# Sorted experts of a fused transformer step: rows loaded from ACT's queue, five raw weight places, results scattered to token rows per tile, the shared down product in two halves

## The reference, cut to what matters

```python
logits = xf @ router_w
probs = jax.nn.softmax(logits, axis=-1)
topw, topi = jax.lax.top_k(probs, K)                      # K = 2 of E = 8
combine = zeros((n, E)).at[arange(n)[:, None], topi].add(topw)
h = silu(einsum('nd,edf->nef', xf, w1))                   # w1, w2: 8 x 512 x 512
ye = einsum('nef,efd->ned', h, w2)
routed = einsum('ne,ned->nd', combine, ye)
gate, up = split(xf @ shared_gate_up)
shared = sigmoid(xf @ shared_gate_w) * ((silu(gate) * up) @ shared_down)
x = x + routed + shared
```

## Time and profile before

| | us |
|---|---|
| median of three runs (1823.58 to 1836.29) | 1834.05 |
| the profiled execution, its own time | 1833.97 |
| its span (first to last instruction) | 1832.2 |
| PE busy over the span | 1648.9 (90%) |
| DVE busy | 941.8 (51%) |
| ACT busy | 646.2 (35%) |
| first product of the tile loop starts | 1606.73 |
| last product of the tile loop ends | 1799.08 |

### The profile page before, as it was taken

One profiled execution on the slowest core, in us unless ns is written; L12 is line 12 of the kernel. 1 busy time (PEld: TensorE's weight loads), 2 busy tenths in 40 slices (PEclk: granted clock), 3 DMA queues, 4 the chain that ended last, 5 costly groups with the idle time before them and its releaser, 6 DMA issues.

```text
span 1832.2 us, 37869 instructions
## 1 busy us (share of the span) xinstructions
PE 1648.9 (90%) x16852; PEld 1324.9 (72%) x16852; DVE 941.8 (51%) x1370; ACT 646.2 (35%) x1138; POOL 139.8 (8%) x144
## 2 busy tenths in 40 slices
PE   4988789999888999988999999999989888778887
PEld 3733677887666788877888888888777666666765
DVE  4331774336336465563555555555551465566765
ACT  2212053234434321123333333333325112366761
POOL 1200520001000000030000000000021000300003
PEclk9999899999889899999999999999989899999999
DMA  5198001111100111111111111111111000589884
GB/s 206 59 372 323 3 24 52 46 47 52 47 25 4 47 47 46 52 55 46 54 53 54 54 54 54 54 42 36 44 37 47 30 4 2 195 301 326 298 296 155
DMA packets 60129, 171.43 MB, mean 94 GB/s; under 512 B 6432, under 2 KB 23328, under 8 KB 49600
## 3 DMA queue, kind: packets, MB, share of 16 engines
q1 hardware_dynamic: 57408, 160.62, 25.3%
q0 software_dynamic: 2560, 8.39, 1.4%
HBM read 150.57 MB, written 18.35 MB: 92 GB/s over the span
## 4 chain that ended last, share of the span: by engine, by line
PE 72%; DVE 10%; issue 6%; ACT 5%; DMA 5%; POOL 2%; SPq 1%; POOLq 0%; DVEq 0%; ACTq 0%
PE PS L775 20%; PE PS L777 19%; PE PS L776 19%; DMA pool_area<-xs_dram 3%; PE PS L1151 2%; PE PS L1006 2%; PE PS L1120 2%; PE PS L882 1%; PE PS L903 1%; DVE Wl L1727 1%; PE PS L1153 1%; DVE bns L1662 1%; PE PS L1135 1%; ACT Wh L1290 1%; ACT SCP L1324 1%
## 5 line engine op out<-in xcount | busy, mean ns | idle before, releaser
L775 PE MATMUL PS<-T1h,Wh 128*128 128x512 f32 x512 | 208.6, 408 | 23.6 <-DVE T1l L1740 11.7
L776 PE MATMUL PS<-T1l,Wh 128*128 128x512 f32 x512 | 205.7, 402 | 0.0
L777 PE MATMUL PS<-T1h,Wl 128*128 128x512 f32 x512 | 205.6, 402 | 0.0
L1727 DVE TENSOR_TENSOR Wl<-W,Wh 128x2048 fp32r<-128x2048 f32 x58 | 132.8, 2291 | 109.8 <-ACT Wh L1290 109.8
L1290 ACT CAST Wh<-W 128x2048 fp32r<-128x2048 f32 x58 | 110.7, 1910 | 121.9 <-PE PS L777 110.9
L1600 POOL TENSOR_TENSOR rs<-ve,half 128x1 f32<-128x1 f32 (+1 forms) x64 | 46.8, 731 | 1386.3 <-DVE ve L1677 1060.3
L775 PE MATMUL PS<-CTh,Wh 128*128 128x256 f32 x512 | 148.0, 289 | 0.6 <-ACT SCP L1488 0.6
L776 PE MATMUL PS<-CTl,Wh 128*128 128x256 f32 x512 | 144.6, 282 | 0.0
L777 PE MATMUL PS<-CTh,Wl 128*128 128x256 f32 x512 | 144.5, 282 | 0.0
L775 PEld LDWEIGHTS PS<-T1h,Wh 128*128 128x128 f32 x512 | 100.5, 196 | 46.6 <-DVE T1l L1740 12.8
L2083 DVE COPY pool_area<-PS 128x512 f32<-128x512 f32 x64 | 44.3, 691 | 165.7 <-PE PS L777 165.7
(11 more groups left out here) (319 smaller groups left out, 3365.2 us busy)
## 6 DMA issues: line engine op xcount, KB each, us to landing
W<-units_dram SPq DMA_DIRECT2D x58, 1024.0 KB, 5.1
pool_area<-units_dram SPq DMA_DIRECT2D x23, 1024.0 KB, 6.5
pool_area<-ctx_t_dram SPq DMA_DIRECT2D x32, 512.0 KB, 4.0
T1f<-ctx_dram SPq DMA_DIRECT2D x25, 512.0 KB, 6.6
H<-ctx_t_dram SPq DMA_DIRECT2D x15, 516.0 KB, 7.9
T1f<-ctx_t_dram SPq DMA_DIRECT2D x12, 516.0 KB, 7.8
xs_dram<-pool_area SPq DMA_DIRECT2D x23, 256.0 KB, 2.3
pool_area<-xs_dram SPq DMA_DIRECT2D x23, 256.0 KB, 5.5
```

What stands on the lines that cost most here:

```text
L775: nc.tensor.matmul(out_, a[0], b[0], start=first, stop=False)
L776: nc.tensor.matmul(out_, a[0], b[1], start=False, stop=False)
L777: return nc.tensor.matmul(out_, a[1], b[0], start=False, stop=last)
L1727: nc.vector.tensor_tensor(low_w(u), raw(u), high_w(u).bitcast(F32), ALU.subtract).then_inc(w_split, 1)
```

## The change

What it does:

1. **Rows.** The tiles of rows are loaded by DMAs that ACT issues (`load_tile`), each right after ACT's high part of the tile that had the place. ACT, no longer SP, waits for the scatters to land.
2. **Raw places.** Five in place of four (NRAW = 5): the fifth is `SCP`. The high and low places stay four. The loads of the loop's second, third and fourth unit wait for DVE's last low part of `su` instead of its last product.
3. **Results.** POOL scatters each result tile to `yt_dram`, row by row, to row k*1024 + token. For that, the slots have to know their tokens: DVE computes `idx2` (five small instructions), POOL scatters 16 times 128 entries of 8 bytes into `meta_dram` and loads them back as `of_slot`. Padding slots go to rows of their own.
4. **End.** SP waits for the last scatter and loads the two results of all tokens in 8 DMAs of 512 KB (into `H` and `pool_area`); DVE then does 16 weighted additions. The 16 gathers are gone.
5. **Down product.** `5.down` is loaded twice: once ahead of the loop, for token tiles 0 to 3 between `su` and the first tile, and once more at the end for tiles 4 to 7.
6. **Ahead of the loop.** `pos` comes one piece of `sg` earlier on PE, and ACT's two small exponentials come three silu pieces earlier, with one ACT_TABLE_LOAD more there and the one inside the loop's first tile gone.

The core of the diff:

```diff
+NRAW = 5
+    for t in range(TG):
+        J.add(("os", t), "dve", unit="5.down")
     J.add(("xt", 0), "dve", split=True)
...
-    for t in range(T):
-        J.add(("os", t), "dve", unit="5.down")
+    for t in range(TG, T):
+        J.add(("os", t), "dve", unit="5.down.again")
...
+        W6s = SCP[:, :, :]
...
+        def raw_slot(u):
+            return u % NW if u < TILE0 else (u - TILE0 + 1) % NRAW
...
             def load_unit(u):
-                if before_in_slot(u) is not None:
-                    sp.wait_ge(w_split, before_in_slot(u) + 1)
+                if earlier(u, raw_slot) is not None:
+                    sp.wait_ge(w_split, earlier(u, raw_slot) + 1)
                 elif u >= TILE0:
-                    sp.wait_ge(tmp_ready, tmps["su", G - 1, C - 1])
+                    sp.wait_ge(dve_drained, J.drain["su", G - 1, C - 1][1])
...
             sp.wait_ge(eid_ready, 1)
-            for k in range(NW6):
-                load_unit(TILE0 + k)
-            sp.wait_ge(scattered, 16 * TOP * T)
-            for i in range(NXS):
-                load_tile(i)
-            for k in range(NW6, 2 * NW6):
-                load_unit(TILE0 + k)
-            for i in range(NT + 1):
-                if i >= 1:
-                    load_tile(i + NXS - 1)
...
-                    store_tile(i - 1)
...
+            for u in range(TILE0, len(UNITS)):
+                load_unit(u)
+            for n in range(NYS):
+                sp.wait_ge(ys_out[n], 16 * len(range(n, NT, NYS)))
+            sp.wait_ge(w_split, len(UNITS))
+            for t in range(0, T, 2):
+                for k, dst in enumerate((H, A2t)):
+                    src = yt_dram[k * TOK + t * P:k * TOK + (t + 2) * P, :].rearrange("(t p) d -> p t d", p=P)
+                    sp.dma_start(dst[:, t:t + 2, :], src).then_inc(y_in[t // 2], 16)
...
+            act.wait_ge(scattered, 16 * TOP * T)
+            for i in range(NXS):
+                load_tile(i)
+            for k in range(2):
                 split_high(TILE0 + k)
...
                 if i + 1 < NT:
                     high_tile(("xt", i + 1), XTh, i + 1)
+                    load_tile(i + 1 + NXS)
...
+            for t in range(T):
+                for k in range(TOP):
+                    nc.gpsimd.indirect_dma_start(slots, bass.IndirectOffsetOnAxis(idx2[:, k, t:t + 1], 0),
+                                                 whose[:, k, t, :], None).then_inc(meta_scattered, 16)
+            pool.wait_ge(meta_scattered, 16 * TOP * T)
+            nc.gpsimd.dma_start(of_slot[:, :, :], meta_dram.rearrange("p (i n) -> p i n", n=2)).then_inc(of_slot_in, 16)
+            pool.wait_ge(of_slot_in, 16)
+            for i in range(NT):
+                pool.wait_ge(act_drained, y_copied(i))
+                nc.gpsimd.indirect_dma_start(yt_dram, bass.IndirectOffsetOnAxis(of_slot[:, i, 0:1], 0),
+                                             YS[:, i % NYS, :], None).then_inc(ys_out[i % NYS], 16)
```

More of the change, by code:

```diff
@@ L112, in tile_order @@
     return order + [("w2", NT - 1)]
-UNITS += [f"6.{w}.{i}" for w, i in tile_order()] + ["5.down"]
-DOWN_ROW = TILE0
-EXPERT_ROW = TILE0 + 1
+UNITS += [f"6.{w}.{i}" for w, i in tile_order()] + ["5.down.again"]
+EXPERT_ROW = TILE0
 UNIT = {name: i for i, name in enumerate(UNITS)}
@@ L431, in build @@
         drained = {"act": act_drained, "dve": dve_drained}
-        w_full = [sem(f"w_full{i}") for i in range(NW6)]
+        w_full = [sem(f"w_full{i}") for i in range(NRAW)]
+        whose_in = sem("whose_in")
+        whose_ready = sem("whose_ready")
+        meta_in = sem("meta_in")
+        meta_zeroed = sem("meta_zeroed")
+        meta_scattered = sem("meta_scattered")
+        of_slot_in = sem("of_slot_in")
+        y_in = [sem(f"y_in{i}") for i in range(T // 2)]
+        x_done = sem("x_done")
         zero_made = sem("zero_made")
@@ L441, in build @@
         ys_out = [sem(f"ys_out{i}") for i in range(NYS)]
-        gathered = [sem(f"gathered{i}") for i in range(T)]
-        gather_used = sem("gather_used")
         small_high = sem("small_high")
@@ L581, in slot, with earlier @@
         def slot(u):
[L583 removed]
+            return u % NW if u < TILE0 else (u - TILE0 + 1) % NW6
+        def raw_slot(u):
+            return u % NW if u < TILE0 else (u - TILE0 + 1) % NRAW
+        def earlier(u, place):
+            return max((v for v in range(u) if place(v) == place(u)), default=None)
         def fills(u):
[L587 to L590 removed]
+            return sum(raw_slot(v) == raw_slot(u) for v in range(u + 1))
         def before_in_slot(u):
[L594 to L596 removed]
+            return earlier(u, slot)
         def raw(u):
[L599 to L600 removed]
+            s = raw_slot(u)
+            return W[:, s, :, :] if s < NW else W6[:, s - NW, :, :] if s < NRAW - 1 else W6s
         def high_w(u):
@@ L1232, in _, with shared_out @@
                 feature_major(("su",), w, T1, g)
+            def shared_out(unit, tokens):
+                w = wait_unit(unit)
+                for t in tokens:
+                    wait(("su", t // TG, C - 1))
+                    token_major(("os", t), w, B1, t)
+            shared_out("5.down", range(TG))
             def transpose_rows(key, src):
@@ L1266, in _ @@
                     transpose_rows(("mt", i), HS[:, i % NHS, :])
-            w = wait_unit("5.down")
-            for t in range(T):
-                wait(("su", t // TG, C - 1))
-                token_major(("os", t), w, B1, t)
+            shared_out("5.down.again", range(TG, T))
         @block.scalar
@@ L1577, in _ @@
             high_tile(("xt", 0), XTh, 0)
+            load_tile(NXS)
+            for k in range(2, NW6):
+                split_high(TILE0 + k)
             for i in range(NT + 1):
@@ L2151, in _ @@
             last_slot, both, first_slot = (tiny[:, 8, i * T:(i + 1) * T] for i in range(3))
-            slot_w = [tiny[:, 9, k * T:(k + 1) * T] for k in range(TOP)]
+            part_of, cell = tiny[:, 9, 0:TOP * T], tiny[:, 10, 0:TOP * T]
+            slot_w = [tiny[:, 13, k * T:(k + 1) * T] for k in range(TOP)]
             dve.wait_ge(dis_in, 16)
@@ L2197, in _ @@
             low_tmp(("su", G - 1, C - 1), B1, (A_, C - 1, grp(G - 1)), G * C - 1)
-            for k in range(NW6):
-                split_low(TILE0 + k)
             def low_tile(key, pair, i):
                 low(key, pair, (A_, i % 2, A_))
+            split_low(TILE0)
+            for t in range(2):
+                weighted(("os", t), t, E)
+            split_low(TILE0 + 1)
+            for t in range(2, TG):
+                weighted(("os", t), t, E)
             low_tile(("xt", 0), (XTh, XTl), 0)
+            for k in range(2, NW6):
+                split_low(TILE0 + k)
             for i in range(NT + 1):
```

118 lines of the change are left out of this document (65 added, 53 removed).

## The result

| | before | changed |
|---|---|---|
| time, median (lowest to highest), same chip | 1835.17 us (1823.58 to 1842.43), 4 runs | 1789.80 us (1788.70 to 1792.57), 4 runs |
| ratio, 95% interval | 1 | 0.9737 (0.9707 to 0.9766) |
| profiled execution: its time, its span | 1833.97, 1832.2 us | 1792.57, 1789.6 us |
| lead: last row factor on POOL to first m1 | 62.2 us | 64.7 us |
| loop: first m1 to last matmul of m2 | 191.9 us (8.34 a tile) | 151.7 us (6.60 a tile) |

The kernel became 2.6% faster, 45 us, where 27 us (1834 to 1807) was forecast; the time lies 2 us under the range.

A forecast was written before the change was run, and what follows sets the result against it. Rows issued late behind SP's waits bound the loop, with the DMA engines next. 1833.97 + 1.4 (units) - 19 (loop) - 3 (after the last load) - 6.6 (end) gave 1806.8, say 1807 us; range 1792 to 1827.

The forecast's parts named there:

- The ring: Tile loop: SP issues rows only behind a unit waiting for a split; PE waited 46.9 us for rows.
- the loop's -19: Tile loop: 173 us of full DMA work at a share of 1, against 192; range -6 to -25 us.
- the rival at 1792 us: Tile loop: engines run at 388 GB/s and PE's 6.5 to 6.9 us a tile set the pace; chance 0.13.
- its units' wait: Start of the loop's loads: units wait for the last low part of `su` instead of the last product, +1.4 us.
- the stretch after the last load: Last tile: rows already there, last weights set the end, about 11.5 us where it was 14.4: -3 us.
- The first m1, priced at nothing: Ahead of the loop: added split and down products fall into gaps, first m1 stays at about 1606.7, no cost.
- The end: Last product to end of span: 33.1 us falls to 26.5, with 16 additions of 0.75 us; -6.6 us.
- The fifth place, priced at nothing by itself: Raw weight places in the loop: four would still be enough, so nothing, up to a few us of share.
- ACT's issue of the rows: Tile loop: at 0.43 us a load no cost; at 1.5 us the loop loses 9 us of its gain.
- The small scatters' work on the engines: Building the slots' list: 2048 packets of 8 bytes take 1.4 to 6.9 us of full work; +3 us taken.
- The rival at 1855 us: Small scatters are late, result scatters queue behind them and ACT stops at the fourth copy; chance 0.06.
- The rival of no change: Tile loop: engines stay at 0.87, the rows' wait becomes an equal units' wait; 1827 to 1833 us; chance 0.30.

The follow-up runs named there:

- the three edits of before: The kernel before with one edit each: rows on ACT's queue (1804.06 us), rows a tile earlier on SP's queue (1796.44 us), five raw places (1809.27 us).
- the run with less work for PE: The changed kernel with only the first of three partial products of each tile's matmuls, all loads, splits and copies kept: 1780.65 us, loop 148.1 us.
- the try with shared additions: Changed kernel with raw places reordered to load the second unit earlier, and four of 16 final additions moved to ACT and POOL: 1791.81 us, end 29.7 us.

## Why the prediction was wrong, and where it was right

**The ring: right.** Rows were late because of where SP could issue them. Asking for them a tile earlier on the same queue gave 38.3 of the 40.2 us. The forecast had put the cure in the queue as well as in the time; the runs say that it is the time.

**The step that failed: 306 / 0.87 = 352 GB/s as what a full share moves.** The prediction read the share of the DMA engines as a filling level that bytes follow in proportion. From it came 7.3 us a tile, "the DMA engines come next, ahead of ACT, PE and DVE", and the loop's -19. Block 0, in the prediction's own rows, had already moved more than that, 388 GB/s. With 415 GB/s, a tile's 2.62 MB take 6.3 us, less than PE's 6.43, and PE sets the loop: that is the rival at 1792 us, to which I had given a chance of 0.13. The trace of before could have told it. These are windows of one microsecond in its loop (columns as above), three with the engines at work on several transfers, three of another kind:

```profile
1654.00:1655.00 1.00, 1.00 (x6) 0.83 (x5) 1.00 (x2) 1.00 (x1) 0.00 (x0) 1.00 0.98 412
1656.00:1657.00 1.00, 0.24 (x2) 0.24 (x3) 1.00 (x1) 0.60 (x1) 0.00 (x0) 1.00 1.18 135
1661.00:1662.00 1.00, 1.00 (x6) 0.82 (x5) 1.00 (x1) 1.00 (x2) 0.00 (x0) 1.00 1.01 426
1676.00:1677.00 1.00, 1.00 (x4) 0.81 (x3) 0.33 (x1) 0.64 (x1) 0.00 (x0) 0.50 0.99 406
1680.00:1681.00 1.00, 1.00 (x6) 0.82 (x5) 0.40 (x1) 1.00 (x1) 0.00 (x0) 1.00 0.63 107
1685.00:1686.00 1.00, 1.00 (x8) 0.85 (x7) 1.00 (x1) 0.75 (x2) 0.00 (x0) 1.00 1.08 143
```

A share of about 1 goes with 406 to 426 GB/s and with 135 to 143. (Of the 92 windows of one microsecond from 1594 to 1786 with a share of 0.95 or more, 49 moved over 400 GB/s and 11 under 250; a packet is counted whole in the window in which it starts.) In the second kind SP had just issued two transfers, from half a microsecond ahead of the window to its start (1655.53 and 1655.91, 1679.70 and 1680.08, 1684.53 and 1684.92): engines count as busy with packets that hardly move yet. That it is the start-up of a transfer on an empty pool is my reading of the order in time; no run here tests it. What is shown is that the average over 192 us mixed the two kinds, that the division by 0.87 left the second kind in, and that in the changed kernel's steady part it is nearly gone (1.01 and 408 GB/s).

The times of single packets in the traces confirm the size. In before's loop (1594 to 1786 us) most packets of 8 KB took 0.309 us, but 853 of 5764 took over 0.355, half of these 0.57 us or more. What these took beyond 0.309 us is 0.12 of the share; without it the 306 GB/s filled 0.74 of the engines, not 0.87, and that is 413 GB/s for a full share (142 us of full work where the prediction had 167). The same sum over the loops (from 1610 us on) of the changed kernel, the one with rows back on SP's queue and the three edits of before gives 411 to 414 GB/s each time. In the changed kernel's steady part only 105 of 3581 packets were slow. Why they are slow stays open.

The objection that I had raised against the rival, a fifth of the bytes in rows of 2 KB, cost little: a packet of 2 KB took 0.084 us, 9% more for its bytes than one of 8 KB, and with these rows in the mix the engines still gave 412 to 417.

The Trainium skill's page "Perfetto Trace Analysis" (Identifying the Most-Contended Engine) warns of just this: for the DMA take the throughput, since occupancy over 16 engines misleads. Its section Roofline names some 435 GB/s of the 16 engines together as the limit of a single active core. The runs agree with both: no 90 us of any run moved more than some 420 GB/s. The figure of about 358 GB/s that the prediction took from the Trainium skill's page "DMA: Bandwidth & Descriptors" (Specifications) lies below what was measured.

**The sum, term by term.** From the last row factor on, 44.9 us were gained where 27.2 were forecast: 17.7 more.
- The loop with its units' wait and the stretch after the last load: forecast +1.4 - 19 - 3, -20.6; measured -40.2. The missing 19.6 us are the whole miss and more. Of the -3, the last unit of a tile landed at 1747.39, 16 us ahead of the last product, and no product waited for a load there: that stretch went at PE's pace as well.
- The first m1, priced at nothing: +2.5 in the profiled execution and +3.7 in the second one. But four other kernels with the same start had 62.5 to 66.2 us, so it lies between nothing and 4 us; its cause, the second unit behind the low part of `su`, was in the prediction as the +1.4. The scatters did start earlier, 26.1 us behind the last row factor in place of 28.8, as forecast; what that gives by itself was not run.
- The end: forecast -6.6 to 26.5 us, measured -7.2 to 26.3, with additions of 0.75 us as priced. Right, and the runs show that it needs both edits.
- The fifth place, priced at nothing by itself: right beside early rows (0.6 us of the loop), wrong as a general statement, since alone it is worth 23 us.
- ACT's issue of the rows, priced at 0.43 us and up to 1.5: 0.326 us, at most 0.454. No cost, right.
- The small scatters' work on the engines, +3 us: the trace has them as 256 packets of 64 bytes, not 2048, which took 3.9 us of one engine, 0.24 us of all 16. Nothing, then, and the kernel without them has the same loop (151.8 against 151.7). Their time on POOL: 1595.6 to 1623.1 us in place of 1591 to 1612, and the first result scatter at 1632.95 in place of about 1624 against the 1637 that was named as the limit. The rival at 1855 us did not happen, but its margin was thinner than 0.06 suggests, as the run with less work for PE showed.

**The rival of no change** asked whether the wait for rows would turn into one for units. It did not: ACT waits for units 5.9 us in all, all of it ahead of the first m1. The tens of us that the forecast itself had named as its sign did not come either, since the loads were not the limit.

## What to carry to other kernels

Look first at how many tiles ahead of its use a late transfer is asked for; one index in an in-order queue was worth nearly as much in this loop as a new queue, a new buffer and a new path together. Judge room on the DMA engines by the GB/s of short windows in which several transfers are under way, never by bytes divided by busy share. And take two edits that break the same ring as one: each alone shows more than half of the gain, and a fifth place beside early rows adds almost nothing.

## What the runs showed of the hardware that I had not expected

GpSimd and VectorE slow each other, but not in every pairing. In the changed kernel, one result scatter (128 rows of 2 KB) held POOL for 0.96 us where DVE was idle, and about 1.97 us in the loop (the columns: start, duration, idle before):

```profile
1644.44 1.97 POOL L1688 DMA_INDIRECT yt_dram<-pool_area,of_slot  x1 [4.46 <-ACT pool_area L1626]
...
1764.61 0.96 POOL L1688 DMA_INDIRECT yt_dram<-pool_area,of_slot  x1 [3.94 <-ACT pool_area L1626]
```

It cost nothing there: POOL idled up to 4.5 us ahead of each, and DVE's subtractions of a unit took 2.28 to 2.29 us with a scatter beside them (26 of them) and 2.29 without (22). In the try with shared additions it did cost: with POOL's additions beside them, DVE's took 1.64 to 1.75 us in place of 0.75, so that both engines together did in 1.7 us two additions, what DVE alone does in 1.5. The Trainium skill's page "SBUF — State Buffer" (SBUF: two separate sides) says that VectorE operations with two inputs from SBUF and GpSimd operations that read it take a shared pair of ports in turns, each for its whole length. The trace agrees: DVE's three slow additions end at 1785.18, 1786.86 and 1788.52, each 0.54 to 0.55 us behind the end of one of POOL's (1784.63, 1786.31, 1787.98). Whether the scatter's second microsecond has the same cause is open: no run here took VectorE's work away under a scatter in the loop.

The pace of a full DMA engine hangs on the packet: 0.309 us for 8 KB, 0.159 for 4 KB, 0.084 for 2 KB, which is 424, 412 and 390 GB/s for 16 engines. Block 0's 388 GB/s, by which the rival had been priced, came from packets of 2 KB and a little over 4 KB.

The time from issue to landing says little on whether a transfer is late: from before to the changed kernel its median grew from 6.5 to 8.2 us for the units in the places that only the tiles use, and from 5.5 to 7.4 us for the rows, while the wait for the rows went away.
